# A four-layer graph network on one core: ScalarE's channel step in four pieces around the node factors, GpSimd's scores ahead of its node values, the last ELU inside the first full step

## The reference, cut to what matters

```python
def _L0_gnn_ref(h, W, a, adj):              # layer 0: graph attention
    Wh = jnp.einsum('bni,io->bno', h, W)
    s1 = Wh @ a1; s2 = Wh @ a2
    e = jax.nn.leaky_relu(s1[:, :, None] + s2[:, None, :], negative_slope=ALPHA)
    e = e + mask[None, :, :]
    attention = jax.nn.softmax(e, axis=2)
    return jax.nn.elu(jnp.einsum('bnm,bmo->bno', attention, Wh))

def _L1_gnn_ref(x, w0, b0, wa, ba, adj):    # layer 1: one softmax for each channel
    feat = jax.nn.softplus(x * (INV_SQRT2 * w0[0, 0]) + b0[0])
    scores = feat * wa + ba
    logits = jnp.where(mask[None, :, :, None], scores[:, None, :, :], -1e9)
    attn = jax.nn.softmax(logits, axis=2)
    return jnp.einsum('bijd,bjd->bid', attn, feat)
```

## Time and profile before

| | us |
|---|---|
| median of 3 runs | 2030.87 (2029.8 to 2031.35) |
| the profiled execution, its own time | 2025.69 |
| span in the profile | 2023.9 |
| mean granted clock of PE | 0.984 of full |

### The profile page before, as it was taken

One profiled execution on the slowest core, in us unless ns is written; L12 is line 12 of the kernel. 1 busy time (PEld: TensorE's weight loads), 2 busy tenths in 40 slices (PEclk: granted clock), 3 DMA queues, 4 the chain that ended last, 5 costly groups with the idle time before them and its releaser, 6 DMA issues.

```text
span 2023.9 us, 95064 instructions
## 1 busy us (share of the span) xinstructions
PE 1913.9 (95%) x43624; PEld 1570.6 (78%) x43624; DVE 1682.9 (83%) x2007; ACT 1233.4 (61%) x1842; POOL 1062.6 (53%) x754
## 2 busy tenths in 40 slices
PE   8888689989999999999999999999999999989998
PEld 6776589987777777777777777777777777767887
DVE  6988769867788888888888888888888888868998
ACT  5776455526666666666666666666666666654342
POOL 6787687723244445454444554545545445454653
PEclk7999889999999999999999999999999999999999
DMA  7000000001111111111111111111111111101111
GB/s 180 4 4 3 3 2 2 2 12 34 34 34 34 34 34 33 35 34 32 35 28 37 31 33 34 33 34 34 34 34 34 34 34 34 34 13 24 25 25 34
DMA packets 88255, 61.24 MB, mean 30 GB/s; under 512 B 45616, under 2 KB 86832, under 8 KB 87856
## 3 DMA queue, kind: packets, MB, share of 16 engines
q1 hardware_dynamic: 85632, 54.57, 11.1%
q10 hardware_dynamic: 2224, 0.59, 0.1%
HBM read 8.98 MB, written 4.19 MB: 7 GB/s over the span
## 4 chain that ended last, share of the span: by engine, by line
PE 69%; DVE 12%; POOL 9%; ACT 4%; issue 3%; DMA 1%; SPq 1%; ACTq 0%; POOLq 0%; DVEq 0%
PE ACC L1580 30%; PE S L1761 23%; PE S L1740 5%; DVE ring L1354 4%; PE AX L1804 3%; PE AX L1813 2%; PE AX L1781 2%; DVE ring L1210 2%; POOL sp_log L766 1%; POOL ln_sq L769 1%; PE AX L1560 1%; POOL below L626 1%; DVE ch_rden L1339 1%; ACT ring L1011 1%; PE AX L1570 1%
## 5 line engine op out<-in xcount | busy, mean ns | idle before, releaser
L1580 PEld LDWEIGHTS ACC<-V,ring 128*64 128x64 f32 x28672 | 957.5, 139 | 190.5 <-DVE ring L1210 38.7
L1354 DVE TENSOR_TENSOR ring<-ring,mask_self_t 128x1024 f32<-128x1024 f32 x640 | 895.0, 1408 | 190.6 <-ACT ring L1011 185.8
L1580 PE MATMUL ACC<-V,ring 128*64 128x65 f32 x28672 | 976.3, 223 | 38.6 <-DVE ring L1210 19.6
L1011 ACT ACTIVATE ring<-S,dot_bias 128x1024 f32<-128x1024 f32 x640 | 713.3, 1115 | 409.4 <-PE S L1761 373.2
L1761 PE MATMUL S<-FA 128*64 128x512 f16 x5120 | 666.0, 382 | 1.4 <-DMA FA<-lo 1.2
L1761 PEld LDWEIGHTS S<-FA 128*64 128x64 f16 x5120 | 253.5, 110 | 161.0 <-ACT ring L1011 15.8
L1210 DVE SCALAR_TENSOR_TENSOR ring<-S,pair_q,mask_t 128x1024 f32<-128x1024 f32 x256 | 315.1, 1272 | 14.4 <-DVE f_max L1222 3.8
L782 POOL TENSOR_TENSOR EV_both<-score,recip 128x512 f32<-128x512 f32 x64 | 124.3, 1942 | 318.1 <-DVE score L1363 318.0
L1740 PE MATMUL S<-parts,mask_t 128*128 128x128 bf16 x3072 | 176.6, 221 | 15.1 <-DVE X L1343 14.2
L1740 PEld LDWEIGHTS S<-parts,mask_t 128*128 128x128 bf16 x3072 | 174.6, 99 | 16.9 <-issue 15.9
L775 POOL TENSOR_TENSOR V<-v_pairs,bh_bc 128x512 f32<-128x512 f32 x64 | 96.5, 1508 | 117.7 <-ACT v_pairs L1031 117.7
(11 more groups left out here) (131 smaller groups left out, 2010.9 us busy)
## 6 DMA issues: line engine op xcount, KB each, us to landing
FA<-hi SPq DMA_DIRECT2D x320, 64.0 KB, 2.0
FA<-lo SPq DMA_DIRECT2D x320, 64.0 KB, 2.0
X<-in_x SPq DMA_DIRECT2D x16, 256.0 KB, 5.0
ring<-in_adj SPq DMA_DIRECT2D x8, 512.0 KB, 8.2
out_x<-X SPq DMA_DIRECT2D x16, 256.0 KB, 2.6
wh<-in_wh_t ACTq DMA_DIRECT2D x2, 64.0 KB, 6.5
bh_bc<-in_bh ACTq DMA_DIRECT2D x1, 128.0 KB, 9.4
w_gat<-in_w_gat ACTq DMA_DIRECT2D x4, 16.0 KB, 3.7
```

The costliest lines, as they stand in the source:

```text
L1011: act.activation(ring[:, jt, :], S[jt % 2][:, :], ACT.Exp, bias=dot_bias[:, n % 2:n % 2 + 1])\
L1354: dve.tensor_tensor(ring[:, jt, :], ring[:, jt, :], mask_self_t[:, jt, :], ALU.mult)\
L1580: last = pe.matmul(acc_of(t)[rows, :], ring[:, jt, t * P + c * CUT:t * P + (c + 1) * CUT], values, start=(jt == 0 and t % 4 == 0), stop=(j ...
```

## The change

It reorders instructions on three engines and touches no operand, tile or instruction. PE's list stays as it is.

- **ACT, units 11 to 15.** The step at the unit's end becomes four pieces. `channel_argument` (976, 980, 982, 984) moves up to just behind `h_t`, ahead of the node factors. `channel_softplus` (986, 988) and `channel_exponent` (992, 997) come just behind the node factors, ahead of `gat_below`. Only `channel_squares` (1001) stays at the end.
- **POOL, units 11 to 15.** The scores (739, 742) move ahead of the node values (642). `channel_norm` (593, 598, 584, 754) stays where the step was. In unit 15 the scores of step 0 come ahead of the addition of graph 14.
- **DVE, units 11 to 15.** Parts 2 and 3 move from behind `jt` = 5 and 6 to behind 6 and 7; the ELU of the previous graph now stands behind part 3.
- **Behind unit 15.** What is left of graph 15 goes inside step 0: on DVE the reciprocal behind part 0 and the ELU behind part 3; on ACT `gat_below` behind the softplus; on POOL the addition behind the whole of `channel_norm`.

```diff
 # POOL, gat_layer
+                    steps = steps_beside(cur)
                     if cur + 1 < B:
                         node_biases(layer, cur + 1)
+                    for k in steps:
+                        channel_score(k, k % 2)
                     if cur + 1 < B:
                         node_values(layer, cur + 1)
...
-                    steps = steps_beside(cur) if layer == 0 else []
                     for k in steps:
-                        channel_step(k, k % 2)
+                        channel_norm(k, k % 2)
+                    if cur == B - 1:
+                        channel_score(0, 0)
                     if cur > 0:
                         gat_add(layer, cur - 1)
...
                 gat_divide(layer, B - 1)
-                gat_add(layer, B - 1)
...
+            def channel_step(k, par):
+                if k > 0:
+                    channel_score(k, par)
+                channel_norm(k, par)
+                if k == 0:
+                    gat_add(0, B - 1)
 # ACT, gat_layer
+                    for k in steps_beside(cur):
+                        channel_argument(k, k % 2)
                     if late_stats(layer, cur) is not None:
                         late_shifts(late_stats(layer, cur))
                     if cur + 1 < B:
                         gat_factors(layer, cur + 1)
+                    for k in steps_beside(cur):
+                        channel_softplus(k, k % 2)
+                        channel_exponent(k, k % 2)
                     if cur > 0 and layer == 0:
                         gat_below(cur - 1)
...
-                    for k in steps_beside(cur) if layer == 0 else []:
-                        channel_step(k, k % 2)
+                    for k in steps_beside(cur):
+                        channel_squares(k, k % 2)
                 gat_sums(layer, B - 1)
-                if layer == 0:
+
+            def channel_step(k, par):
+                channel_argument(k, par)
+                channel_softplus(k, par)
+                if k == 0:
                     gat_below(B - 1)
-
-            def channel_step(k, par):
+                channel_exponent(k, par)
+                channel_squares(k, par)
 # DVE, gat_layer
+                        if layer == 0 and jt in (1, 3, 6, 7):
+                            for k in steps_beside(cur):
+                                channel_part(k, k % 2, (1, 3, 6, 7).index(jt))
                         if jt == 7 and cur > 0 and layer == 0:
                             gat_elu(cur - 1)
-                        if layer == 0 and jt in (1, 3, 5, 6):
-                            for k in steps_beside(cur):
-                                channel_part(k, k % 2, (1, 3, 5, 6).index(jt))
-                gat_reciprocal(layer, B - 1)
-                if layer == 0:
+
+            def channel_step(k, par):
+                channel_part(k, par, 0)
+                if k == 0:
+                    gat_reciprocal(0, B - 1)
+                channel_part(k, par, 1)
+                channel_part(k, par, 2)
+                channel_part(k, par, 3)
+                if k == 0:
                     gat_elu(B - 1)
-
-            def channel_step(k, par):
-                for part in range(4):
-                    channel_part(k, par, part)
                 channel_result(k, par)
```

More of the change, by code:

```diff
@@ L732, in last_layer, with channel_score @@
                 gat_add(3, B - 1)
-            def channel_step(k, par):
+            def channel_score(k, par):
                 b = k + 2
@@ L743, in channel_step, with channel_norm @@
                         .then_inc(ch_score, 1)
+            def channel_norm(k, par):
                 b = k + 4
@@ L964, in gat_layer, with channel_argument @@
                         late_squares(late_stats(layer, cur))
-                    for k in steps_beside(cur) if layer == 0 else []:
-                        channel_step(k, k % 2)
+                    for k in steps_beside(cur):
+                        channel_squares(k, k % 2)
                 gat_sums(layer, B - 1)
-                if layer == 0:
+            def channel_step(k, par):
+                channel_argument(k, par)
+                channel_softplus(k, par)
+                if k == 0:
                     gat_below(B - 1)
-            def channel_step(k, par):
+                channel_exponent(k, par)
+                channel_squares(k, par)
+            def channel_argument(k, par):
                 b = k + 1
@@ L984, in channel_step, with channel_softplus @@
                     act.activation(relu_z[:, :], zt[:, :], ACT.Relu, bias=b0_c[:, :], scale=w0_c[:, :]).then_inc(ch_relu, 1)
+            def channel_softplus(k, par):
+                b = k + 3
+                if exists(b):
                     act.wait_ge(ch_az, b + 1)
@@ L988, in channel_step, with channel_exponent @@
                     act.activation(sp_log[:, :], sp_log[:, :], ACT.Ln, bias=1.0).then_inc(ch_log, 1)
+            def channel_exponent(k, par):
                 b = k + 1
@@ L997, in channel_step, with channel_squares @@
                     act.activation(EV[:, :, D:2 * D], tiles(score[:, :]), ACT.Exp).then_inc(ch_e, 1)
+            def channel_squares(k, par):
                 b = k + 5
```

## The result

The changed kernel takes 2017.2 us (median of 4 runs, 2014.72 to 2018.15), the kernel before 2030.34 us (4 runs, 2027.69 to 2031.35). The ratio is 0.9932 with an interval of 0.992 to 0.9945: 13 us faster. Forecast were 2013.2 us with 2007.5 to 2020.0.

A forecast was written before the change was run, and what follows sets the result against it. PE bounds the kernel, but stands still in units 13 to 15 and layer 1's first steps, waiting on DVE, ACT and POOL. Gains of 10.3 + 4.6 + 2.8 = 17.7 us from 2030.87 gave 2013.2 us, range 2007.5 to 2020.

The forecast's parts named there:

- the sum's own worst case of 13.6: Whole kernel: at worst 7.8 + 3.0 + 2.8 = 13.6 us gained, a time of 2017.3 us.
- the prediction's own signs of being wrong: Softplus behind DVE's `jt` = 6, line 976 over 13 us behind step 0, or step 4's lead missing at the end.
- 3.95 + 2.99 + 3.26 = 10.20 us earlier at step 0: Units 13, 14 and 15: DVE's three waits for ACT vanish, bringing step 0 forward 10.20 us.
- I take 10.3 us, the middle: Gain at step 0 after DVE and POOL waiting for each other, between 7.8 and 12.3 us.
- the worst case of 7.8: Step 0: 12.3 us less 4.5 us of new meetings between DVE and POOL leaves 7.8 us.
- hidden beside the last tile's product: nothing: Unit 15: DVE's third part, 1.21 us on PE's path to step 0, is covered and costs nothing.
- I take 12: Step 1: POOL's product of graph 2 comes 12 us behind PE's step 0, within 9.9 to 13.6.
- the worst end of 13.6: Step 1: the latest arrival of POOL's product of graph 2, 13.6 us behind PE's step 0.
- 2.8 is on the harmless side: PE's 2.8 us gap before step 2 keeps full clock, so steps 2 to 4 gain 2.8 us.
- the clock still falls in step 2: Rival: PE's gap is 4.4 us, 2.8 us not gained, 2017.6 us; chance 0.19 shared with a remaining wait.
- the lead is kept through layer 1: Behind step 4: steps hang on the two before, not a date; layers 2 and 3 start earlier by the same.
- Slower: meetings eat more than the waits gave: Rival, units 13 to 15 and step 0: some 18 DVE operations meeting POOL erase 17.7 us from 1.0 each; chance 0.03.

The follow-up runs named there:

- the minimum on ACT: The changed kernel with POOL's minimum with 0 moved to ACT for graphs 12 to 15 of layer 0; 2012.05 us, ratio 0.9909 to before.
- the parts behind 5 and 6: The changed kernel with DVE's parts 2 and 3 back behind tiles 5 and 6, ELU still last; 2015.18 us, ratio 0.993 to before.
- The run with filled gaps: The changed kernel with unread products in PE's gaps behind steps 1 and 14 and in layer 2's first features; 2016.41 us, ratio 0.9923 to before.
- the units alone: The kernel before with all of the change inside units 11 to 15, the order behind unit 15 as before; 2020.92 us, ratio 0.9956.
- the end alone: The kernel before with only the new order behind unit 15, step 0's scores drawn into unit 15; 2022.23 us, ratio 0.9967.

## Why the prediction was right, and where its sum was off

The time is inside the range, and the direction and the mechanism hold: DVE stood for ACT's late step, and ACT's pieces alone give 8.4 us where the change gives 13. The forecast itself was 4 us too low. Up to step 4 the traces give 12.3 us, less than the sum's own worst case of 13.6; the 2017.2 us of the runs lie just at that case's 2017.3.

Two of the prediction's own signs of being wrong came. Line 976 of step 1 (now 999) starts 13.5 us behind step 0, where more than 13 was the sign. And of the 12.3 us of lead at step 4 only 10.5 are left at the end of the traces, where a constant lead was said. Term by term:

- **"3.95 + 2.99 + 3.26 = 10.20 us earlier at step 0": right.** All three waits are gone from the trace.
- **"I take 10.3 us, the middle": too much; 7.4 came, under the worst case of 7.8.** The meetings of DVE and POOL were mis-sized. I let the old ones vanish and gave new ones 0 to 4.5 us; 5.4 us were measured. The two large ones that I hadn't priced are `feat` (0.8) and the third part (1.1) of unit 15. Meetings don't vanish when both engines get fuller.
- **The third part "hidden beside the last tile's product: nothing": wrong in the trace.** It took 2.32 us against a product of 1.15, and PE stood 1.19 us. Putting it back gained nothing measurable, so what it costs in time isn't settled.
- **"I take 12" for POOL's product of graph 2: 13.5, close to the worst end of 13.6.** The start of `o` was inside its bounds, 3.1 us behind step 0. POOL's way from there to the end of the product took 10.3 us, where I had 7.9 to 9.2, as the division, the minimum and the scaling of line 598 (2.06 us) met DVE. From line 999 to step 2 it took 12.3 us, not 12.7. The gain from step 0 to 2 was 3.6 us instead of 4.6. The run with the minimum on ACT shows that POOL sets this.
- **"2.8 is on the harmless side": the step that failed.** The gap came out at 4.2 us, and the clock fell for part of step 2 (0.77 from 273 to 279): 1.4 us gained instead of 2.8. It is the rival "the clock still falls in step 2" (2017.6 us), at half its price: with a late product it had a gap of 4.4 us. The reasoning was wrong too. Two gaps of the kernel before (3.34 and 3.72 us) don't give a limit between them: a gap of 2.50 us was followed by a step pair of 23.23 us (the parts behind 5 and 6), one of 2.61 us by 21.60 (the minimum on ACT).
- **"the lead is kept through layer 1": but for 1.4 us.** Step 15 took 11.92 us at a lower clock behind gaps like those in front of step 15 before, where it took 10.88. The other 0.4 us are the products just ahead of step 15. The run with filled gaps shows that it is the clock.
- **The sum:** 17.7 us forecast; 7.38 + 3.56 + 1.40 = 12.34 in the traces up to step 4. That this is near the 13 us of the runs is in part chance: over their whole spans the two traces differ by 8.9 us, and executions of one kernel by up to 8.6.
- **"Slower: meetings eat more than the waits gave": no.** At some 0.8 us each they took back a third, near the price measured before the change. The scores ahead of the node values, costed at nothing, brought nothing that shows in the run of the units alone. Graph 15's late addition was run only as a part of the end's new order, so its own cost isn't shown.
- **Reordering in units 11 and 12: not costed at all.** Unit 12 was 1.75 us longer in the change's trace, at a lower clock. Whether the change causes it stays open.

## What to carry to other kernels

When a wait is taken away, look at the engine that becomes full by it: here DVE was 12 us idle, and 3 of these came back as waits against POOL, whose share nobody had lightened. An instruction moved within a full engine, or from one full engine to the other, gained nothing measurable in three tries; one taken to an engine with room gained 5 us in four graphs and 10 more in the other twelve. Products that fill a gap have to fit into it: when the gap closes by another edit, they are work on the path. And a single profile can't judge an edit of 2 us where two engines meet by chance: the same order up to step 0 was 2.4 us apart in two of them.

## What the runs showed of the hardware

- A DVE instruction of 0.17 us on 128x8 elements took up to 1.23 us when it met a POOL instruction. The Trainium skill (SBUF — State Buffer, "Who interferes with whom") counts scalings with one tensor among the operations that can take the ports shared with GpSimd, when their operands meet its conditions. These rows agree that they contend.
- POOL's power doesn't hold DVE up. The row of the prediction shows only 0.27 us of overlap, but in the change's step 2 a whole `feat` took 0.69 us, its time alone, inside the power:

```profile
274.03 2.49 POOL L593 TENSOR_TENSOR ln_rstd<-ln_ve,neg_half 128x8 f32<-128x8 f32 x1 [0.17 <-DVE ln_ve L1232]
```

```profile
275.76 0.69 DVE L1360 TENSOR_TENSOR feat<-relu_z,sp_log 128x512 f32<-128x512 f32 x1
```

- PE's clock isn't told by the gap's length alone: steps behind gaps of 1.63 and 2.61 us ran at full clock, pairs behind 2.50, 3.22 and 4.16 us took 1.4 to 1.6 us longer. A gap of 6.77 us made a pair of 24.38 us in the kernel before, one of 6.76 us a pair of 22.99 with all of the units. Steps 15 behind the same two gaps (0.82 and 1.5 us) took 10.88 us in some kernels and 11.84 to 12.27 in others. What else decides isn't settled.
- Executions of one kernel spread over up to 8.6 us (2019.22 to 2027.85 for the end alone; 2025.03 to 2033.3 for the kernel before), which is over half of what this change brought.
